# Gate and up of a gated FFN by seven products instead of eight blocks, with the FFN's first step ahead of the attention's last output

## The reference

```python
x = x + tanh(g_xattn[0]) * xattn(layernorm(x), ctx, ctx, Wq, Wk, Wv, Wd)
def ffn(x, ...):
    a = x @ (gate_w * (gate_su @ gate_sv)).T      # 512 -> 1792
    b = x @ (up_w * (up_su @ up_sv)).T            # 512 -> 1792
    return (silu(a) * b) @ (down_w * (down_su @ down_sv)).T
x = x + tanh(g_ffn[0]) * ffn(layernorm(x), ...)
```

## Time and profile before

| | us |
|---|---|
| median of 3 runs (1588.8 to 1590.08) | 1589.48 |
| the profiled execution, its own time | 1590.0 |
| its span, first to last instruction | 1588.2 |
| PE busy | 1554.6 (98%) |
| DVE busy | 932.9 (59%) |
| ACT busy | 465.1 (29%) |
| POOL busy | 434.7 (27%) |
| mean granted TensorE clock | 0.989 |

### The profile page before, as it was taken

How to read it: one execution, slowest core, us unless ns; L and a number is a source line. 1 busy time by engine, 2 the same in 40 slices (tenths; PEclk the granted TensorE clock), 3 DMA queues, 4 the chain that set the end, 5 groups by cost and what they waited for, 6 DMA issues and landing times.

```text
span 1588.2 us, 20950 instructions
## 1 busy us (share of the span) xinstructions
PE 1554.6 (98%) x8010; PEld 1302.5 (82%) x8010; DVE 932.9 (59%) x1436; ACT 465.1 (29%) x810; POOL 434.7 (27%) x378
## 2 busy tenths in 40 slices
PE   7999989999999899999999999998999999999999
PEld 7898877778888788888888888886888888888887
DVE  4155468987778577676777777687633323333333
ACT  3123235544444232232323232233221212212121
POOL 0122379887788010000000010016300101101010
PEclk9999999999999899999999999998999999999999
DMA  6456557768987423232332323241001001010002
GB/s 227 142 159 227 171 195 248 247 221 288 354 289 243 165 81 125 80 126 80 126 105 96 113 86 120 82 138 64 0 1 40 21 20 40 0 41 20 20 27 80
DMA packets 107570, 194.96 MB, mean 123 GB/s; under 512 B 8784, under 2 KB 46928, under 8 KB 106448
## 3 DMA queue, kind: packets, MB, share of 16 engines
q1 hardware_dynamic: 107472, 193.63, 36.4%
HBM read 128.06 MB, written 65.54 MB: 122 GB/s over the span
## 4 chain that ended last, share of the span: by engine, by line
PE 95%; DVE 2%; DMA 1%; POOL 1%; issue 0%; ACT 0%; DVEq 0%; ACTq 0%; POOLq 0%
PE bank L404 71%; PE bank L625 9%; PE bank L520 7%; PE bank L549 4%; PE bank L534 2%; PE bank L460 1%; DMA k_scratch<-k_st 1%; PE bank L573 0%; PE bank L452 0%; DVE el L926 0%; POOL gu_lo L1190 0%; POOL xn L1183 0%; DVE q_st L968 0%; DMA c_raw<-in_ctx_t 0%; DMA v_scratch<-v_st 0%
## 5 line engine op out<-in xcount | busy, mean ns | idle before, releaser
L404 PE MATMUL bank<-wd_hi,o_hi 128*128 128x512 f32 x512 | 208.6, 407 | 2.1 <-ACT o_hi L762 2.1
L404 PE MATMUL bank<-wd_hi,o_lo 128*128 128x512 f32 x512 | 201.0, 392 | 0.0
L404 PE MATMUL bank<-wd_lo,o_hi 128*128 128x512 f32 x512 | 200.8, 392 | 0.0
L1038 DVE TENSOR_TENSOR d_sb<-bank,s_sb 128x512 f32<-128x512 f32 x56 | 38.7, 692 | 259.3 <-ACT s_sb L793 259.3
L404 PE MATMUL bank<-xc_hi,wa_hi 128*128 128x512 f32 x448 | 176.4, 394 | 6.2 <-DVE q_st L968 3.1
L404 PE MATMUL bank<-xc_hi,wa_lo 128*128 128x512 f32 x448 | 175.0, 391 | 0.0
L404 PE MATMUL bank<-xc_lo,wa_hi 128*128 128x512 f32 x448 | 174.9, 390 | 0.0
L404 PE MATMUL bank<-xt_hi,gu_hi 128*128 128x512 f32 x448 | 174.5, 389 | 0.0
L404 PE MATMUL bank<-xt_hi,gu_lo 128*128 128x512 f32 x448 | 174.3, 389 | 0.0
L404 PE MATMUL bank<-xt_lo,gu_hi 128*128 128x512 f32 x448 | 174.3, 389 | 0.0
L1175 POOL TENSOR_TENSOR wd_lo<-wd_raw,wd_hi 128x512 fp32r<-128x512 f32 x32 | 41.4, 1293 | 467.1 <-ACT wd_hi L745 467.1
(11 more groups left out here) (116 smaller groups left out, 3205.5 us busy)
## 6 DMA issues: line engine op xcount, KB each, us to landing
q_scratch<-q_st SPq DMA_DIRECT2D x32, 1024.0 KB, 4.4
q_sb<-q_scratch SPq DMA_DIRECT2D x64, 512.0 KB, 3.3
wq_raw<-in_wq SPq DMA_DIRECT2D x32, 512.0 KB, 4.4
er_raw<-in_sf_r SPq DMA_DIRECT2D x42, 256.0 KB, 3.0
e_raw<-in_wf SPq DMA_DIRECT2D x42, 256.0 KB, 5.0
ffn_eff_scratch<-e_eff SPq DMA_DIRECT2D x42, 256.0 KB, 4.8
f_raw<-ffn_eff_scratch SPq DMA_DIRECT2D x14, 768.0 KB, 4.6
k_scratch<-k_st SPq DMA_DIRECT2D x32, 256.0 KB, 3.6
```

Of the source, the lines that this page charges most:

```text
L404: last = pe.matmul(to, a, b, start=(start and n == 0), stop=(stop and n == 3 * len(pairs) - 1), skip_group_check=onto)
L1038: v.tensor_tensor(d_sb[t][:, :], bank[2 * (1 - t) + 1][:, :], s_sb[t][:, :], ALU.mult).then_inc(v_m, 1)
```

## The change

Gate and up are now made by the same seven-product scheme as the queries. The two rows of blocks are gate and up, the inner dimension is split into halves of 256, and the columns are two sets of 512 tokens. A step n (0 to 27) is one inner tile (n modulo 14) for one half of the tokens (1024): `gate_up(n)` is seven products of 6 matmuls, in the order 1, 6, 5, 4, 2, 7, 3, and `down(n)` is 8 token tiles of 3 matmuls. The order on PE is gate_up(n), down(n - 1). The weights are loaded, summed and split again for each half of the tokens (28 times instead of 14), and the down results of two inner tiles are no longer added up in PSUM: DVE adds 8 tiles to `X` in every step.

The normalised x is no longer kept as 4 column blocks but as 7 (the blocks and their sums), 1792 columns to a group: `x2_columns` (ACT copies to `xb2`), `x2_sums` (four subtractions of 256 columns, on POOL for groups 0 to 3, on DVE for groups 4 to 7), `x2_hi_of` (ACT) and `x2_lo_of` (DVE). Groups 0 to 3 (the first half of the tokens) are done in the attention loop, groups 4 to 7 in the FFN steps: `stats2` at the end of steps 0, 1, 2 and 4 (`ROWS2`), `columns2` inside steps 1, 2, 3 and 5 (`COLUMNS2`). The attention loop ends one turn earlier, and the two outputs of the last unit come behind gate_up(0), in banks 4 and 5. The split of the first weights moves from turn 60 to turn 58 of that loop.

```diff
+NF = NB * NJ
...
-    xt_hi = at(79, "xt_hi", [P, KC, T], F32R)
-    xt_lo = at(111, "xt_lo", [P, KC, T], F32R)
-    xn2 = at(143, "xn2", [P, 2, D])
...
+    xn2 = at(135, "xn2", [P, 2, D])
+    xb2 = at(139, "xb2", [P, 8, 2, P])
+    x2_hi = [at(79, "x2_hi0", [P, 4, 7, 2, P], F32R), at(147, "x2_hi1", [P, 4, 7, 2, P], F32R)]
+    x2_lo = [at(107, "x2_lo0", [P, 4, 7, 2, P], F32R), at(55, "x2_lo1", [P, 4, 6, 2, P], F32R)]
+    x2_lo_last = at(203, "x2_lo_last", [P, 4, 1, 2, P], F32R)
...
+    wf_hi = at(175, "wf_hi", [P, 7, 2, P], F32R)
+    wf_lo = at(182, "wf_lo", [P, 7, 2, P], F32R)
+    f_raw = at(189, "f_raw", [P, 2, D])
+    fs = at(193, "fs", [P, 4, 2, P])
...
+    ROWS2 = {0: 4, 1: 5, 2: 6, 4: 7}
+    COLUMNS2 = {n + 1: m for n, m in ROWS2.items()}
...
+        def load_f(n):
+            j = n % NJ
+            if n:
+                sp.wait_ge(g_fw, 3 * n)
+            sp.dma_start(f_raw[:, :, :], ed[3 * j:3 * j + 2].rearrange("n p d -> p n d")).then_inc(d_f, 16)
+        def load_down(n):
+            if n:
+                sp.wait_ge(g_dn, n)
+            sp.dma_start(dn_raw[:, :], ed[3 * (n % NJ) + 2]).then_inc(d_dn, 16)
...
-            three_pass(bank[t][:, :],
+            three_pass(bank[t if u < NU - 1 else 4 + t][:, :],
...
-        for i in range(1, NU + 2):
+        for i in range(1, NU + 1):
...
-            if 60 <= i:
+            if 60 <= i < 64:
...
-        def gate_up(u, t):
-            gate_or_up(u, t, 0)
-            gate_or_up(u, t, 1).then_inc(p_g[t], 1)
...
-        pe.wait_ge(v_xt2, 12)
-        gate_up(0, 0)
-        columns2(6, (4, 5))
-        pe.wait_ge(v_y, 2 * NU)
-        gate_up(0, 1)
-        columns2(7, (6, 7))
-        gate_up(1, 0)
-        pe.wait_ge(v_xt2, TT)
-        for u in range(NIG * NFC):
-            if u >= 1:
-                if u >= 2:
-                    gate_up(u, 0)
-                down(u - 1, 1)
-                gate_up(u, 1)
-            down(u, 0)
-        down(NIG * NFC - 1, 1)
+        def ffn_product(n, number, to, a, b, onto=False):
+            blk = n // NJ
+            lo = x2_lo_last[:, :, 0] if blk == 1 and b == 6 else x2_lo[blk][:, :, b]
+            three_pass(bank[to][:, :].rearrange("p (s t) -> p s t", s=4),
+                       [((wf_hi[:, a, k, :], wf_lo[:, a, k, :]), (x2_hi[blk][:, :, b, k, :], lo[:, :, k, :]))
+                        for k in range(2)], start=not onto, onto=onto).then_inc(p_f[number], 1)
+        def gate_up(n):
+            if n % NJ == 0:
+                pe.wait_ge(a_x2hi, 4 * (n // NJ + 1))
+                pe.wait_ge(v_x2lo, 4 if n == 0 else 12)
+            pe.wait_ge(a_fw, 3 * n + 1)
+            pe.wait_ge(g_fw, 3 * n + 1)
+            if n:
+                pe.wait_ge(a_silu, 2 * n - 1)
+            else:
+                pe.wait_ge(v_y, 2 * (NU - 1))
+            ffn_product(n, 1, 0, 0, 0)
+            pe.wait_ge(a_fw, 3 * n + 3)
+            pe.wait_ge(g_fw, 3 * n + 3)
+            if n:
+                pe.wait_ge(v_f2, n)
+            ffn_product(n, 6, 1, 4, 4)
+            if n:
+                pe.wait_ge(v_f12, n)
+            else:
+                pe.wait_ge(a_xt2, 8)
+            ffn_product(n, 5, 2, 3, 3)
+            if n:
+                pe.wait_ge(v_f21, n)
+            ffn_product(n, 4, 3, 2, 6)
+            if n in COLUMNS2:
+                if n == 1:
+                    pe.wait_ge(v_y, 2 * NU)
+                else:
+                    pe.wait_ge(v_yf, 8 * (n - 1))
+                columns2(COLUMNS2[n], (4, 5))
+            pe.wait_ge(a_f1, n + 1)
+            ffn_product(n, 2, 0, 1, 1, onto=True)
+            pe.wait_ge(v_f1, n + 1)
+            ffn_product(n, 7, 1, 5, 5, onto=True)
+            pe.wait_ge(a_f5, n + 1)
+            ffn_product(n, 3, 2, 6, 2, onto=True)
+        def down(n):
+            pe.wait_ge(a_dn, n + 1)
+            pe.wait_ge(g_dn, n + 1)
+            pe.wait_ge(v_d, 2 * n + 2)
+            b = d_buffer(n)
+            if n + 1 in COLUMNS2:
+                pe.wait_ge(a_xt2, 2 * COLUMNS2[n + 1] + 2)
+            for k in range(8):
+                half, cols = k // 4, slice(k % 4 * P, (k % 4 + 1) * P)
+                if 8 * n + k >= 4:
+                    pe.wait_ge(v_yf, 8 * n + k - 3)
+                elif k >= 2:
+                    pe.wait_ge(v_add if k == 2 else a_pt, NU)
+                to = bank[4 + k % 4][:, :]
+                pe.matmul(to, d_hi[b][:, half, cols], dn_hi[:, :], start=True, stop=False)
+                pe.matmul(to, d_hi[b][:, half, cols], dn_lo[:, :], start=False, stop=False)
+                pe.matmul(to, d_lo[b][:, half, cols], dn_hi[:, :], start=False, stop=True).then_inc(p_yf, 1)
+        gate_up(0)
+        for t in range(2):
+            output(NU - 1, t)
+        gate_up(1)
+        down(0)
+        for n in range(2, NF):
+            gate_up(n)
+            down(n - 1)
+        down(NF - 1)
...
+        def x2_columns(m, banks):
+            a.wait_ge(p_xt2, 2 * m + 1)
+            if m:
+                a.wait_ge(v_x2lo, m if m <= 4 else 2 * m - 4)
...
+        def ffn(n):
+            a.wait_ge(p_f[1], n + 1)
+            if n:
+                a.wait_ge(v_d, 2 * n - 1)
+            a.activation(f1[:, :], bank[0][:, :], ACT.Copy).then_inc(a_f1, 1)
+            if n in COLUMNS2:
+                x2_columns(COLUMNS2[n], (4, 5))
+            a.wait_ge(p_f[5], n + 1)
+            if n:
+                a.wait_ge(v_d, 2 * n)
+            a.activation(f5[:, :], bank[2][:, :], ACT.Copy).then_inc(a_f5, 1)
+            a.wait_ge(p_f[2], n + 1)
+            if n:
+                a.wait_ge(v_m, 2 * n - 1)
+            a.activation(silu[n == 0][:, :], bank[0][:, :], ACT.Silu).then_inc(a_silu, 1)
+            if n + 1 < NF:
+                gate_up_hi(n + 1, 0)
+                gate_up_hi(n + 1, 1)
+            if n in COLUMNS2:
+                x2_hi_of(COLUMNS2[n])
+            d_hi_of(n, 0)
+            if n + 1 < NF:
+                gate_up_hi(n + 1, 2)
+            a.wait_ge(v_f12, n + 1)
+            a.activation(ft1[:, :], ft1[:, :], ACT.Silu).then_inc(a_silu, 1)
+            d_hi_of(n, 1)
+            down_hi(n)
...
+            if 60 <= i < 64:
+                x2_columns(i - 60, (2, 3))
+                x2_hi_of(i - 60)
...
+        def x2_lo_of(m):
+            blk, s = m // 4, m % 4
+            v.wait_ge(a_x2hi, m + 1)
+            for to, part in [(x2_lo[0], slice(0, 7))] if blk == 0 else [(x2_lo[1], slice(0, 6)),
+                                                                        (x2_lo_last, slice(6, 7))]:
+                v.tensor_tensor(to[:, s].rearrange("p n k t -> p (n k) t"),
+                                xb2[:, 1 + part.start:1 + part.stop, :, :].rearrange("p n k t -> p (n k) t"),
+                                f32(x2_hi[blk][:, s, part]).rearrange("p n k t -> p (n k) t"),
+                                ALU.subtract).then_inc(v_x2lo, 1)
...
+        def gated(n):
+            v.wait_ge(p_f[7], n + 1)
+            if n:
+                v.wait_ge(g_c22, n)
+            v.tensor_tensor(ft2[:, :], bank[1][:, :], f1[:, :], ALU.add).then_inc(v_f2, 1)
+            v.wait_ge(v_f2, n + 1)
+            v.tensor_tensor(f1[:, :], ft2[:, :], bank[3][:, :], ALU.subtract).then_inc(v_f21, 1)
+            v.wait_ge(v_f21, n + 1)
+            v.wait_ge(a_silu, 2 * n + 1)
+            v.tensor_tensor(f1[:, :], f1[:, :], silu[n == 0][:, :], ALU.mult).then_inc(v_m, 1)
+            v.wait_ge(p_f[3], n + 1)
+            v.tensor_tensor(ft1[:, :], bank[2][:, :], ft1[:, :], ALU.add).then_inc(v_f12, 1)
...
+        def gated_second(n):
+            v.wait_ge(a_silu, 2 * n + 2)
+            v.wait_ge(g_c22, n + 1)
+            v.tensor_tensor(f5[:, :], f5[:, :], ft1[:, :], ALU.mult).then_inc(v_m, 1)
...
+        for n in range(NF):
+            ffn_sums(n)
+            if n in COLUMNS2:
+                x2_sums(COLUMNS2[n])
+            gated(n)
+            if n == 0:
+                for t in range(2):
+                    add_to_x(NU - 1, t)
+            if n >= 2:
+                add_ffn(n - 1, range(4))
+            if n in COLUMNS2:
+                x2_lo_of(COLUMNS2[n])
+            d_lo_of(n, 0)
+            gated_second(n)
+            if n >= 2:
+                add_ffn(n - 1, (4, 5))
+            d_lo_of(n, 1)
+            if n >= 1:
+                add_ffn(n - 1, (6, 7) if n >= 2 else range(8))
+            if n in ROWS2:
+                stats2(ROWS2[n])
+        add_ffn(NF - 1, range(8))
...
+        def ffn(n):
+            if n + 1 < NF:
+                ffn_left_sums(n + 1)
+                ffn_left_lo(n + 1, 0)
+            if n:
+                second_up(n)
+            if n + 1 < NF:
+                ffn_left_lo(n + 1, 1)
+                ffn_left_lo(n + 1, 2)
+            if n == 0:
+                second_up(n)
+            down_lo(n)
...
-            if i == NU - 4:
-                ffn_lo(0)
-            if 59 <= i:
+            if i == NU - 6:
+                ffn_left_sums(0)
```

(14 more changed lines are left out.)

327 lines of the change are left out of this document (159 added, 168 removed).

## The result

| | before | after |
|---|---|---|
| median, us (4 runs each, same chip) | 1589.78 | 1623.6 |
| ratio, 95% interval | | 1.0212 [1.0195, 1.023] |
| span of the profiled execution | 1588.2 | 1620.1 |
| mean granted TensorE clock | 0.989 | 0.977 |

The kernel became 2.1% slower. 1603 us was predicted, with 1584 to 1622 as the range: the sign is right, the size is not, and the time lies 1.6 us beyond the range. The sum was made for the span and gave 1602.5, so 17.6 us have to be found.

The account below looks back on a forecast made before the run. PE's matmul count was taken as the bound: 1125.4 + 424.6 matmuls + 3.2 transposes + 29.9 stalls + 3.4 to the end = 1586.5, with 16 of clock 1602.5; by the median, 1603 us. Range 1584 to 1622.

Parts of the forecast that it names:

- A steady step: FFN steps: PE has 15.0 us of matmuls and stays the bound; tightest wait product 6, with 1.7 us to spare.
- Port: DVE operations with two SBUF inputs and POOL reading SBUF exclude each other; four per step, which DVE can afford.
- third rival: Steady steps late through POOL, held by DVE: 1.1 us in each of 22 steps, 24 us, 1628 us; chance 0.10.
- The gain: Gate and up need 168 fewer matmuls at 0.227 us each, worth 38.1 us.
- the price that no row shows: Gate and up's moving operands in four runs of 128 columns: taken as nothing, at most 46 us.
- fourth rival: Gate and up's four-run operands cost their upper bound: 1650 us; chance 0.04.
- The end of attention: Last attention turns: normalised tiles come at 1079.5, 1094.5 and 1109.5 us, and step 0 starts at 1125.4.
- this ring: End of attention: next group's statistics wait for this group's tiles, through softmax, copies and subtractions; 15.0 us a turn against 9.83.
- The stalls: PE's waits in steps 1, 2, 3, 5, 6, down(0) and the last down product: 29.9 us in sum.
- The clock: PE's clock falls to half after long waits: five stretches at 3.2 us, 16 us; bounds none and 38 us.
- The first rival: The stalls come but PE's clock holds: 1587.8 us, no difference; chance 0.11.
- The second rival: Late groups' chain from statistics to transposes takes 5 us instead of 7.75, so faster: 1575 us; chance 0.17.

Follow-up runs that it names:

- the first experiment: The changed kernel with DVE's join of the second gate half moved behind the four adds of the down product: 1610.63 us, ratio 1.0146.
- the four edits: The changed kernel with second join behind the adds, late groups' statistics earlier, POOL and splits reordered at attention's end, down(0)'s adds in usual place: 1575.09 us, ratio 0.9924.

## Why the size of the prediction was wrong

**The step that failed** is "A steady step", in the words "the next thing that PE needs of it is the sum before product 7, at E + 5.4 + 6.8". PE needs something of DVE sooner: the bank of the fifth down tile, free after the first add, at E + 2.7. By the prediction's own numbers the first add ends at E + 1.5 + 0.7 = E + 2.2, which leaves 0.5 us; this was the tightest wait, not product 6 with its 1.7. The product then took 1.48 in place of 0.69 us, the add came at about E + 3.0, and 0.48 us were lost in each step. 22 steps at 15.50 in place of 14.98 are 11.4 us; the first experiment got 11.0 back. The "Port" paragraph had the rule that explains it, and the third rival the right kind of loss (1.1 us in each of 22 steps, chance 0.10). But both looked at POOL as the one that is held, and held four DVE operations to be something "which DVE can afford".

**The gain** of 38.1 us is right: 0.227 us apart in both kernels. So is **the price that no row shows**: operands in four runs cost nothing that the rows show, which rules out the fourth rival.

**The end of attention** was right in mechanism and too short in size, and the absolute times hide by how much. The tiles were forecast at 1079.5, 1094.5 and 1109.5 and step 0 at 1125.4; PE's timeline has the transposes of the second tile of each group at 1077.8, 1093.6 and 1109.4, and step 0 at 1127.3:

```profile
1063.80 1.04 PE L597 MATMUL bank<-ident,xn 128*128 128x128 f32 x8
...
1077.80 1.11 PE L597 MATMUL bank<-ident,xn 128*128 128x128 f32 x4 [2.16 <-POOL xn L1312]
...
1093.62 1.10 PE L597 MATMUL bank<-ident,xn 128*128 128x128 f32 x4 [2.16 <-POOL xn L1312]
...
1109.43 1.12 PE L597 MATMUL bank<-ident,xn 128*128 128x128 f32 x4 [2.16 <-POOL xn L1312]
```

But the forecast was made on the times of the kernel before, whose profiled execution reaches the transposes of group 0 (the first row here) 2.8 us later:

```profile
1066.58 1.04 PE L573 MATMUL bank<-ident,xn 128*128 128x128 f32 x8
```

PE has the same work up to there in both, so these 2.8 us are the luck of one execution (those of the experiments lie up to 4.5 us apart there). Counted from there, the tiles were forecast at 12.9, 27.9 and 42.9 us and came at 14.0, 29.8 and 45.6 (a turn of 15.8 us where 15.0 was worked out; 0.3 of it is the subtractions, for which ACT waits 3.5 us where 3.2 was put), and step 0 was forecast at 58.8 and came at 63.5: 4.7 us late, 2.0 of them behind the last tile. Three stretches at half clock stand in this part (13.8 us of busy time); how much of the 4.7 us is theirs isn't shown. Opening this ring brings step 0 forward by 16.0.

**The stalls** came where they were put:

| | forecast | measured |
|---|---|---|
| step 1 | 5.1 | 4.6 |
| down(0) | 4.5 | 6.6 |
| step 2 | 2.4 | 1.6, and 1.3 in down(1) |
| step 3 | 7.0 | 6.7 |
| step 5 | 4.8 | 4.7 |
| step 6 | 3.9 | 3.7 |
| end | 2.2 | 3.2 |
| sum | 29.9 | 32.4 |

Only down(0) is off by much, by 2.1 us, and for the reason above once more. The timeline of DVE and of POOL ahead of its first add:

```profile
1162.23 1.74 DVE L1124 TENSOR_TENSOR x_lo<-xb,x_hi 128x1536 fp32r<-128x1536 f32 x1
1163.90 2.56 DVE L1124 TENSOR_TENSOR x_lo_last<-xb,x_hi 128x256 fp32r<-128x256 f32 x1
```

```profile
1163.40 2.77 POOL L1345 TENSOR_TENSOR wf_lo<-fs,wf_hi 128x1024 fp32r<-128x1024 f32 x1 [1.09 <-ACT wf_hi L852]
```

POOL's split of the weights starts while DVE's first operation runs (until 1163.97) and takes 2.77 us where 2.4 is usual, and DVE's 256 columns end 0.29 us after it. In step 5, with POOL standing still, the same 256 columns took 0.41 us in place of 2.56:

```profile
1260.12 0.41 DVE L1124 TENSOR_TENSOR x_lo_last<-xb,x_hi 128x256 fp32r<-128x256 f32 x1
```

**The clock** cost 14.0 us where 16 was forecast: six stretches of 2.3 us where five of 3.2 were counted. The three at the end of attention are not in the 14.0, since they fall into the time before step 0. The first rival (it holds) is out.

**The sum**: steady steps +11.4, the end of attention +4.7 less the 2.8 of luck ahead of it, stalls +2.5, clock -2.0, and from the last matmul's end to the end 4.0 us in place of 3.4, +0.6. These are 14.4 of the 17.6 us. Of the other 3.2, 1.3 come from how waits are drawn: the bracket counts from a matmul's drawn end, 0.39 us after its start, while the next was due at 0.227, so each of the eight waits behind a 512-column matmul lasted 0.16 longer than its bracket. The last 1.9 were not pinned down; part of it are first matmuls behind a wait, which are followed by the next after 0.34 us and not 0.227. Without the 2.8 us of luck the miss would have been 20.4 us.

One number of the prediction's closing words is wrong by its own terms: the work left over by the end of attention is 5.4 + 1.6 = 7.0 us and not 8.6, which counts 16 transposes that the kernel before has too. The forecast does not use it.

**The second rival** (faster) did not happen in this kernel, since the chain from a group's statistics to its transposes was as long as worked out. The kernel with the four edits got there (1575.09 us), by taking other work from ahead of these chains.

## What to carry to other kernels

When a change makes the bound engine's work shorter, list for each product every buffer and bank that it needs, with the due time and the slack, and take the smallest: here the one with 0.5 us was left out, while the one with 1.7 was watched. Price a VectorE operation with both inputs in SBUF, met by a running GpSimd operation that reads SBUF, as lasting until that one ends and most of its own time more (here 0.55 us of 0.69), and the other way round where GpSimd's comes second. Compare spans from a point up to which the kernels do the same work: here 2.8 us of a miss hid ahead of it. A saving in matmuls is kept only if the order of the small work is remade with it: the same arithmetic cost 2.1% in one order and won 0.8% in another.

## What the runs showed of the hardware beyond what was expected

- A 512-column DVE operation with two SBUF inputs took 1.48, 1.07 or 0.69 us by what POOL did: the two long ones ended 0.55 us after POOL's operation. One of 256 columns took 2.56 us in this way and 0.41 without it.
- It works both ways, by who comes first. In the kernel with the later join, the timeline of DVE has the product 0.2 us ahead of POOL's sum:

```profile
1304.69 0.79 DVE L1145 TENSOR_TENSOR f<-f,silu 128x512 f32<-128x512 f32 x1
```

```profile
1304.89 1.74 POOL L1359 TENSOR_TENSOR f<-ft,f 128x512 f32<-128x512 f32 x1
```

  Here the product takes 0.79 us and POOL's sum 1.74 in place of 1.28, so it was held for 0.46 us.
- A wait of 0.20 us in PE's column cost 0.48 by the distances from start to start, so small waits in every step are read from the step's length, not from the waits.
